# Self-attention's output product: one low tile fewer per eight heads, and lent rows copied in other slots

## The reference

```python
Wdkv = x @ latent_w + latent_b                                  # 72 latents, keys and values at once
q = jnp.einsum('btc,hcl->bhtl', x, Wd_w) + Wd_b[None, :, None, :]   # 16 heads
scores = jnp.einsum('bhtl,bsl->bhts', q, Wdkv) / sqrt(d_head)
attn = jax.nn.softmax(jnp.where(causal, scores, -jnp.inf), axis=-1)
y = jnp.einsum('bhts,bsl->bhtl', attn, Wdkv)
z = jnp.transpose(y, (0, 2, 1, 3)).reshape(b, t, h * 72)
return z @ out_w + out_b                                        # the output product
```

## Time and profile before

| what | us |
|---|---|
| median of 3 runs (3086.27 to 3086.43) | 3086.36 |
| the profiled execution | 3084.58 |
| its span, first to last instruction | 3082.8 |
| TensorE busy (99% of the span) | 3057.7 |
| VectorE busy (73%) | 2255.4 |
| ScalarE busy (70%) | 2162.3 |
| GpSimd busy (51%) | 1579.3 |

### The profile page before, as it was taken

How to read it: one execution, slowest core, us unless ns; L and a number is a source line. 1 busy time by engine, 2 the same in 40 slices (tenths; PEclk the granted TensorE clock), 3 DMA queues, 4 the chain that set the end, 5 groups by cost and what they waited for, 6 DMA issues and landing times. The chain is left out here.

```text
span 3082.8 us, 72822 instructions
## 1 busy us (share of the span) xinstructions
PE 3057.7 (99%) x22529; PEld 2874.0 (93%) x22529; DVE 2255.4 (73%) x6595; ACT 2162.3 (70%) x6949; POOL 1579.3 (51%) x2918
## 2 busy tenths in 40 slices
PE   9999999999999999999999999999999999999998
PEld 7999999999999999999999999999988888889998
DVE  7888888888888777777878778788765555454665
ACT  8888888888888878888888888888844444442222
POOL 5676676666776765333333333333456666652000
PEclk9999999999999999999999999999999999999999
DMA  5455555544444461111111111111354454534333
GB/s 163 137 156 166 155 157 160 150 129 125 119 129 132 129 212 46 46 49 63 46 49 60 52 46 53 59 46 49 110 144 100 99 118 104 113 52 96 123 122 102
DMA packets 209569, 321.06 MB, mean 104 GB/s; under 512 B 36416, under 2 KB 143040, under 8 KB 208224
## 3 DMA queue, kind: packets, MB, share of 16 engines
q1 hardware_dynamic: 184672, 283.59, 30.7%
q0 software_dynamic: 24576, 33.57, 6.6%
HBM read 125.20 MB, written 75.50 MB: 65 GB/s over the span
## 5 line engine op out<-in xcount | busy, mean ns | idle before, releaser
L1214 POOL TENSOR_SCALAR ca_prob<-ca_prob,ca_inverse 128x120 f32<-128x120 f32 x1024 | 354.9, 366 | 623.9 <-DVE ca_inverse L1539 621.8
L875 ACT ACTIVATE sa_prob<-sa_prob,sa_shift 128x128 f32<-128x128 f32 (+1 forms) x1024 | 453.9, 462 | 0.0
L1480 ACT ACTIVATE ca_prob<-bank,ca_shift 128x120 f32<-128x120 f32 x1024 | 353.1, 363 | 1.7 <-DVE ca_shift L1533 0.4
L937 DVE CUSTOM_DVE_ANT_0 sa_prob<-bank,sa_mask 128x128 f32<-128x128 f32 (+1 forms) x1024 | 303.4, 351 | 5.7 <-issue 5.2
L599 POOL TENSOR_SCALAR sa_prob<-sa_prob,sa_inverse 128x128 f32<-128x128 f32 x512 | 195.2, 381 | 200.4 <-DVE sa_inverse L949 187.0
L139 PE MATMUL bank<-sa_kvT_b,sa_q 112*128 112x128 f32 (+1 forms) x1024 | 260.4, 279 | 0.0
L981 DVE TENSOR_TENSOR sa_pT_lo<-bank,sa_pT_hi 128x384 fp32r<-128x384 f32 x512 | 258.2, 544 | 0.2 <-ACT sa_pT_hi L864 0.2
L601 POOL TENSOR_SCALAR sa_prob<-sa_prob,sa_inverse 128x256 f32<-128x256 f32 x512 | 251.3, 491 | 0.0
L137 PE MATMUL bank<-sa_kvT_a,sa_q 128*128 128x128 f32 (+1 forms) x1024 | 249.4, 280 | 1.1 <-DVE sa_shift L937 0.9
L1973 POOL DMA_INDIRECT mid_acc<-ex_out,ex_to_tokens x112 | 191.0, 1705 | 89.0 <-DVE ex_out L2285 60.4
L2163 ACT ACTIVATE ex_act_g<-bank 128x512 f32<-128x512 f32 x128 | 76.5, 598 | 215.8 <-PE bank L132 205.7
(11 more groups left out here) (274 smaller groups left out, 11834.2 us busy)
## 6 DMA issues: line engine op xcount, KB each, us to landing
sa_q<-sa_q_tile SPq DMA_DIRECT2D x125, 288.0 KB
sa_q<-sa_q_tile SPq DMA_DIRECT2D x157, 112.0 KB
mid_x2T<-ca_x2T SPq DMA_DIRECT2D x32, 512.0 KB, 3.0
ex_sx<-mid_x2T SPq DMA_DIRECT2D x32, 512.0 KB, 3.4
sa_q<-sa_q_tile SPq DMA_DIRECT2D x297, 32.0 KB
sa_xT_raw<-in_xT SPq DMA_DIRECT2D x32, 256.0 KB, 3.0
sa_q<-sa_q_tile SPq DMA_DIRECT2D x32, 256.0 KB
sa_x_res<-in_x SPq DMA_DIRECT2D x32, 256.0 KB, 3.5
```

What stands on the lines that cost most here:

```text
L875: act.activation(prob[:, r, hh, cols], prob[:, r, hh, cols], ACT.Exp, bias=shift[:, r, n:n + 1], scale=-1.0, accum_out=total[:, r, n:n + 1 ...
L937: dve.tensor_tensor_reduce(out=prob[:, r, hh, cols], in0=SC[hh][:, t * T:t * T + (t + 1) * P], in1=mask[:].rearrange("p a s -> p (a s)")[: ...
L1214: ins = pool.tensor_scalar(prob[:, r, t, hh], prob[:, r, t, hh], inverse[:, r, n:n + 1], 1.0, ALU.mult, ALU.mult)
L1480: act.activation(prob[:, r, t, hh], SC[g % 2][:, n * S:n * S + S], ACT.Exp, bias=shift[:, r, n:n + 1], accum_out=total[:, r, n:n + 1]).the ...
```

## The change

All four pairs of each half group now share: pair 0 (and 4) lends, pairs 1, 2, 3 (5, 6, 7) hold, each head to the heads of its own parity. So the lender's slots (`lender(g)`, `g % 8 < 2`) have no low tile, and the other six slots of eight have four low matmuls each. Before, of eight slots four had four, two had none and two had six. The four DMAs of a half group each carry two heads instead of one. They have a semaphore of their own per holder (`lent1` to `lent3`), and are issued in slots without a query tile (`LEND`): for pair 0 those for holders 1 and 2 in slot 13 and for holder 3 in slot 15, for pair 4 in slots 4 and 7. `X_NEXT` moves from slot 3 to 1, `RES_IN` from slots 4 and 5 to 0 and 1. DVE writes 72 rows of `y_lo` everywhere; POOL leaves out the lenders' copies.

```diff
+def lender(g):
+    return g % (2 * QUAD) < 2
...
-    X_NEXT, X_SPLIT = 3, (8, 11)
+    X_NEXT, X_FIRST, X_SPLIT = 1, 3, (8, 11)
...
-    RES_IN, RES = (GROUP + 4, GROUP + 5), (GROUP + 6, GROUP + 9)
+    RES_FIRST, RES_IN, RES = (GROUP + 4, GROUP + 5), (GROUP, GROUP + 1), (GROUP + 6, GROUP + 9)
+    LEND = {13: (2, (1, 2)), 15: (4, (3,)), 4: (1, (1, 2)), 7: (4, (3,))}
...
+        def lend(J, m, at):
+            g = m - at[0] - PL
+            if slot_exists(J, g):
+                y, r = y_at(J, g - 1), (g - 1) % RING
+                need_alone(sp, ylo_done, upto_slot(J, g), spare_sp)
+                need(sp, o_mm, upto_slot(J, g - 2))
+                for n in at[1]:
+                    own = y_at(J, g - 1 + 2 * n)
+                    own = slice(own, own + 2)
+                    sp.dma_start(f32(y_lo[L:AT, own]), f32(y_lo[(n - 1) * GAP:n * GAP, y:y + 2])).then_inc(lent[n], 16)
+                    if n == 1:
+                        sp.dma_start(f32(y_lo[P - REST:P, own]), f32(y_hi[0:REST, r:r + 2])).then_inc(lent[n], 16)
...
-            g = m - PL
-            if slot_exists(J, g) and packed(g) and g % QUAD == 1:
...
-                    sp.dma_start(f32(to), f32(frm[rows, at:at + 2, 0])).then_inc(y_in, 16)
-            if u == X_NEXT and group_exists(J, c + 1):
+            if u in LEND:
+                lend(J, m, LEND[u])
+            if u == (X_FIRST if first_body(J) and c == 0 else X_NEXT) and group_exists(J, c + 1):
...
-                need(pe, ydup_done, upto_slot(J, g))
+                need(pe, ydup_done, upto_own(J, g))
...
-                parts = [(y_hi, r, 0, 0), (y_hi, r, 0, 1)]
-                if not packed(g):
-                    parts += [(y_lo, y, 1, 0), (y_lo, y, 1, 1)]
-                elif p % 2 == 1:
-                    parts += [(y_lo, y_at(J, g - 2), 1, -1), (y_lo, y, 1, 0), (y_lo, y, 1, 1)]
-                for part, n, a, hh in parts:
-                    if a == 1 and hh < 0:
-                        need(pe, y_in, upto_quad(J, g, 64))
+                parts = [(y_hi, r, 0)]
+                if not lender(g):
+                    need(pe, lent[p % QUAD], upto_lent(J, g, p % QUAD))
+                    parts += [(y_lo, y_at(J, g), 1)]
...
-                if g % QUAD < 2 and packed(g - QUAD):
-                    need(act, y_in, upto_quad(J, g - QUAD, 64))
+                if lender(g - QUAD):
+                    need(act, lent[1], upto_lent(J, g, 1))
...
-                low = slice(0, L if packed(g) else AT)
+                if lender(g - Y_RING):
+                    for n in range(1, QUAD):
+                        need(dve, lent[n], upto_lent(J, g, n))
+                low = slice(0, L)
```

More of the change, by code:

```diff
@@ L210, in upto_quad, with upto_own, upto_lent @@
     return J * (SA_BODY // (2 * QUAD) * per) + per * (g // (2 * QUAD) + 1)
-def packed(g):
-    return g // QUAD % 2 == 1
+def lender(g):
+    return g % (2 * QUAD) < 2
+def upto_own(J, g):
+    return J * (SA_BODY // (2 * QUAD) * 6) + 6 * (g // (2 * QUAD)) + max(0, g % (2 * QUAD) - 1)
+def upto_lent(J, g, n):
+    return upto_quad(J, g, 32 if n == 1 else 16)
 def y_at(J, g):
@@ L360, in self_attention @@
     ydup_done = al.sem("ydup_done")
-    y_in = al.sem("y_in")
+    lent = {n: al.sem(f"lent{n}") for n in range(1, QUAD)}
     q_mm, qhi_done, qlo_done = al.sem("q_mm"), al.sem("qhi_done"), al.sem("qlo_done")
@@ L551, in slot @@
                         load_ow(p)
-            for c, i in due(J, m, RES_IN):
+            for c, i in due(J, m, RES_FIRST if first_body(J) and m < 2 * GROUP else RES_IN):
                 need(sp, o_read, upto_row(J, c, i - 2))
@@ L603, in slot @@
             g = m - PL
-            if slot_exists(J, g):
+            if slot_exists(J, g) and not lender(g):
                 r = g % RING
@@ L607, in slot @@
                 need_alone(pool, yhi_done, upto_slot(J, g), spare_pool)
-                own = slice(int(packed(g) and g % QUAD < 2), 2)
-                pool.tensor_scalar(y_lo[AT:AT + REST, y_at(J, g), own], f32(y_hi[0:REST, r, own]), 1.0, 1.0, ALU.mult, ALU.mult).then_inc(ydup_done, 1)
-                need(pool, ydup_done, upto_slot(J, g))
+                pool.tensor_scalar(y_lo[AT:AT + REST, y_at(J, g)], f32(y_hi[0:REST, r]), 1.0, 1.0, ALU.mult, ALU.mult).then_inc(ydup_done, 1)
+                need(pool, ydup_done, upto_own(J, g))
             c, u = m // GROUP, m % GROUP
@@ L767, in slot @@
                     need(pe, o_read, upto_row(J, c, i - 2))
-                y = y_at(J, g)
-                parts = [(y_hi, r, 0, 0), (y_hi, r, 0, 1)]
-                if not packed(g):
-                    parts += [(y_lo, y, 1, 0), (y_lo, y, 1, 1)]
-                elif p % 2 == 1:
-                    parts += [(y_lo, y_at(J, g - 2), 1, -1), (y_lo, y, 1, 0), (y_lo, y, 1, 1)]
-                for part, n, a, hh in parts:
-                    if a == 1 and hh < 0:
-                        need(pe, y_in, upto_quad(J, g, 64))
[L777 to L783, removed]
+                parts = [(y_hi, r, 0)]
+                if not lender(g):
+                    need(pe, lent[p % QUAD], upto_lent(J, g, p % QUAD))
+                    parts += [(y_lo, y_at(J, g), 1)]
+                for part, n, a in parts:
+                    rows = slice(0, AT + REST if a == 1 and p % QUAD > 1 else P)
+                    for hh in range(2):
+                        w = slice((2 * p + hh) * C, (2 * p + hh + 1) * C)
+                        for t in range(TT):
+                            tk = slice(t * P, t * P + P)
+                            mm = pe.matmul(O[i][:, t * C:t * C + C], part[rows, n, hh, tk], ow[rows, a, w],
+                                           start=p == 0 and a == 0 and hh == 0 and t == 0, stop=p == NP - 1 and a == 1 and hh == 1,
+                                           skip_group_check=True)
                 mm.then_inc(o_mm, 1)
@@ L904, in split_ow @@
             for a in range(2):
-                cols = slice(C if a == 1 and p % 4 == 2 else 0, 2 * C)
-                dve.scalar_tensor_tensor(out=part[:, a, cols], in0=f32(part[:, a, cols]), scalar=minus_low[:, a:a + 1], in1=raw[:, a, cols],
+                dve.scalar_tensor_tensor(out=part[:, a], in0=f32(part[:, a]), scalar=minus_low[:, a:a + 1], in1=raw[:, a],
                                          op0=ALU.mult, op1=ALU.add).then_inc(ow_done, 1)
@@ L2433, in filled @@
     def filled(h):
-        own, lent, n = ow[:, h * C:(h + 1) * C], ow[:, (h - h % QUAD) * C:(h - h % QUAD + 1) * C], h % QUAD
-        apart = not packed(h)
+        lent_by, n = h - h % (2 * QUAD) + h % 2, h % (2 * QUAD) // 2
+        own, lent = (ow[:, k * C:(k + 1) * C] for k in (h, lent_by))
         rows = np.zeros((P, C), ow.dtype)
-        if n > 0 or apart:
+        if n > 0:
             rows[:L], rows[AT:AT + REST] = own, own[:REST]
-        if n > 0 and not apart:
             rows[L:AT] = lent[(n - 1) * GAP:n * GAP]
-        if n == 2 and not apart:
+        if n == 1:
             rows[AT + REST:] = lent[:REST]
```

## The result

The changed kernel takes 3143.4 us (median of five runs, 3140.7 to 3145.2), against 3086.4 before (3085.1 to 3086.6): a ratio of 1.0184 with a 95% interval of 1.0172 to 1.0196. The forecast was 3120 us with a range of 3100 to 3143: the direction is right, the size is too small by 23 us, and the time lies just outside the range.

A forecast was written before the change was run, and what follows sets the result against it. PE's queue was taken to set the time. Waits of 34.5 us, group 0's 7, groups 3 and 6's 4 and the end's 4, less 15.4, gave +34 on the 3086.36 median: 3120 us, range 3100 to 3143.

The forecast's parts named there:

- What bounds the kernel: Whole kernel: PE's queue sets the time, busy for 3057.7 of 3082.8 us.
- The removed matmuls, -15.4: Output product: 128 of 896 low matmuls go, at 0.12 us each, 15.4 us gained in full unless PE waits.
- The wait in slot 14, 15 x 2.3: Slot 14: PE waits 2.3 us (1.9 to 3.1) per group for the first holder's copies; 15 groups, 34.5 us.
- The prediction's other estimate: Landing of the copies in slot 14: 0.2 us earlier by the skill's fixed DMA cost, the sum 3 us smaller.
- Group 0: Slot 14 of group 0: query tiles come later, so PE waits 7 us instead of 2.3, between 6 and 8.
- Groups 3 and 6: Weights staged ahead of tiles 3 and 7 delay the copies: 4 us for both groups, between 0 and 6.
- the third holder's waits: Second half of groups 3 and 6: DVE's y_lo waits for the copy behind tile 3, 1.1 us in group 3.
- The end, 4 us: Last group: copies in slot 4 land late behind a 1 MB weight load; 4 us, between 0 and 6.
- the clock as a rival: After each of 16 waits: one slot at half clock, 3.6 us more, 58 in all, 3178 us; 4 in 100.
- ACT and DVE have 0.6 us in hand: After slot 14's wait: y_hi and y_lo take 1.3 us from the landing, before PE needs y_lo; no added cost.
- The rival of the spreading wait: Slots 15 or 0: ACT and DVE late, PE waits again, 1 to 1.5 us per group, 3136 to 3144; 11 in 100.

The follow-up runs named there:

- the run with the copies ahead: The changed kernel with the three copies of slot 13 issued in slot 12, ahead of its query tile: 3083.6 us, ratio to before 0.9995.
- either fill: The changed kernel with 26 or 20 matmuls of zeros ahead of PE's wait in slot 14: 3133.9 us with 26, 3135.3 us with 20.

## Why the prediction was right and wrong

- **What bounds the kernel: right.** PE's queue. Every us of wait in it went into the time, and where the waits go, the removed matmuls are gained nearly in full.
- **The removed matmuls, -15.4: right.** The trace has -0.98 a group, 15.7 us in all.
- **The wait in slot 14, 15 x 2.3: right in place and cause, a little short in size.** The copies stand behind tile 7, as the run with the copies ahead shows. In the thirteen regular groups the idle time is 2.49 on the mean, the delay from start to start 2.73; it is 2.50 in groups 8, 9 and 14. In group 13 the landing took 1.95 us where the forecast had 1.77. The prediction's other estimate of it was 0.2 shorter, by the Trainium skill, DMA: Bandwidth & Descriptors (Anatomy of one DMA). That section fits DMAs issued from GpSimd, these are issued by SP, and the measured landing, which decides, is the longer.
- **Group 0: right,** 6.3 for 7. **Groups 3 and 6: right in slot 14,** 7.3 with 4.6 + 4 forecast. But the 4 was also to cover the third holder's waits, which were forecast for groups 3 and 6 alone; slots 5 to 9 cost 7 us more, in groups 2, 3 and 6 above all, and with less regularity than a sum over issues can give.
- **The end, 4 us: right as a mechanism, wrong for this kernel.** The wait is there as soon as the others are taken away (4.03 us); with them it is hidden behind them. I added terms that shorten each other.
- **The clock, left out of the sum: the step that failed.** The sum prices a wait by the delay alone. In eleven of 16 groups PE's clock fell behind the wait, and that cost 19.6 us by slots; without it the time would have been about 3124 us, inside the range. The prediction had the clock as a rival at 4 in 100, at 3.6 us for each of 16 waits; it came, at 1.2 us a group. The reason given against it was that all slices of the trace of before stand at full. They stand at 0.9 or more, which is all that the row can tell. The finer view has 1.00 through self-attention, and the lower clock only at the end of the span, where PE has no matmul left:

```profile
3075.00:3080.00 5.00, 0.00 (x0) 0.00 (x0) 1.54 (x6) 0.00 (x0) 0.68 (x1) 0.58 0.31 105
3080.00:3082.80 2.80, 0.00 (x0) 0.00 (x0) 0.00 (x0) 0.00 (x0) 0.00 (x0) 0.50 0.00 0
```

PE's idle stretches are 1.4 us at most in that trace up to its last matmul, so it couldn't give the price of a longer one. But that was a reason for a term with wide ends, and I left the rival's cheaper versions out of both the sum and the range. The Trainium skill, TensorE: Matmul & The Clock Gate (Part 1), says that the slow clock is the default and activity releases it; the runs agree as far as that the clock mostly stays up when the same wait is filled with matmuls (three falls instead of eleven).

- **ACT and DVE have 0.6 us in hand: right.** Slot 15's excess was the clock's, as the zero matmuls show. The rival of the spreading wait had the right time, 3136 to 3144, for another reason: that is luck.

What stays open is in which groups the clock falls. In the changed kernel it fell after waits of 2.28 and 2.27 us (groups 1 and 2) and not after 2.26 and 2.66 (groups 8 and 4), so the length of the wait alone doesn't decide. No run here holds the length and varies the moment of the wait or what comes before it.

## What to carry to other kernels

A new wait on an engine that is always busy can cost more than the delay: what the engine loses after it, here by the clock, belongs in the sum as a term with its own ends, even where the trace of before shows no such case. A copy that is needed soon after some event should not stand in the queue behind DMAs that wait for that same event: here the order of two blocks in SP's program is worth 60 us, and with the third holder's copies and the late weights it turns a loss of 1.8% into a gain of 0.5%. And a small copy behind large loads in one queue lands with them: 160 KB behind the weights were there 10.9 us after the end of their issue, against 1.95 in group 13.

## What the runs showed of the hardware

The granted clock fell behind idle stretches of TensorE as short as 1.02 us (group 3 with either fill, behind matmuls of zeros) and 1.69 us (group 1 with the wait behind the high matmuls), in some cases and not in others: 1.40 us in the run with the copies ahead and 2.66 in the changed kernel left it up. It stayed down for some us: in that group 1 it was 0.79 and 0.87 of full in two stretches of 5 us, then 1.00. A row that shows the clock in tenths hides all this, since a mean of 0.98 over 1200 us is 24 us.
